# Weighted values of eight heads in one burst, twice a phase, in a two-layer transformer block kernel

## What is computed

```
x = x + attn0(layernorm(x))     # causal, rotary, scores q.k + 0.1 q^2.k^2, output projection with a gate
x = x + ffn0(layernorm(x))      # 128 -> 512, relu, -> 128, biases
x = x + attn1(layernorm(x))     # full attention, biases, no output projection
x = x + ffn1(layernorm(x))      # 128 -> 384 gate and up, silu(gate) * up, -> 128
attend: softmax(scores) @ V per head, 256 queries x 256 keys
```

## Time and profile before

| | us |
|---|---|
| median of three runs | 321.77 |
| the profiled execution | 320.94 |
| its span | 319.0 |
| PE busy | 292.7 |
| DVE busy | 252.6 |
| ACT busy | 217.0 |
| POOL busy | 176.8 |
| L978, the groups' products, busy | 61.7 |

### The profile page before, as it was taken

How to read it: one execution, slowest core, us unless ns; L and a number is a source line. 1 busy time by engine, 2 the same in 40 slices (tenths; PEclk the granted TensorE clock), 3 DMA queues, 4 the chain that set the end, 5 groups by cost and what they waited for, 6 DMA issues and landing times.

```text
span 319.0 us, 8438 instructions
## 1 busy us (share of the span) xinstructions
PE 292.7 (92%) x2852; PEld 209.1 (66%) x2852; DVE 252.6 (79%) x1000; ACT 217.0 (68%) x494; POOL 176.8 (55%) x406
## 2 busy tenths in 40 slices
PE   6769799899999999999999999999999999999945
PEld 4545566677776777777687766776666565655634
DVE  7878988987969877676777776779798989895464
ACT  7661566776676868685867767787778767677621
POOL 5642767778695868687777523527272717170210
PEclk9976799999999999999999999999999999999997
DMA  6977224411313121211212010021312111100001
GB/s 194 340 167 167 66 55 116 117 51 52 108 46 94 44 83 53 85 51 40 73 37 70 22 43 27 25 60 28 77 26 62 42 44 27 44 3 19 17 1 33
DMA packets 23178, 21.59 MB, mean 68 GB/s; under 512 B 2944, under 2 KB 20096, under 8 KB 23136
## 3 DMA queue, kind: packets, MB, share of 16 engines
q1 hardware_dynamic: 23136, 21.05, 23.9%
HBM read 13.18 MB, written 7.34 MB: 64 GB/s over the span
## 4 chain that ended last, share of the span: by engine, by line
PE 51%; DVE 25%; POOL 13%; issue 6%; ACT 4%; POOLq 0%; ACTq 0%; DVEq 0%
PE bank L978 11%; DVE NM L757 7%; PE bank L952 5%; PE bank L1008 4%; PE bank L1021 4%; PE bank L928 4%; POOL XN L430 3%; PE bank L929 3%; POOL RS L423 3%; POOL PB L469 3%; PE bank L956 3%; DVE JUNK L754 3%; PE bank L1067 2%; PE bank L1053 2%; PE bank L875 2%
## 5 line engine op out<-in xcount | busy, mean ns | idle before, releaser
L590 ACT ACTIVATE PB<-bank 128x384 f32<-128x384 f32 (+1 forms) x256 | 134.6, 545 | 47.7 <-PE bank L954 23.9
L757 DVE TENSOR_REDUCE NM<-bank 128x2 f32<-128x512 f32 x128 | 83.8, 684 | 21.0 <-PE bank L929 20.6
L952 PE MATMUL bank<-QS,KS 128*128 128x256 f16 x256 | 70.2, 275 | 2.4 <-ACT PB L590 1.6
L978 PE MATMUL bank<-PB,VP 128*32 128x256 f32 (+1 forms) x1024 | 61.7, 358 | 1.0 <-ACT PB L590 0.9
L754 DVE CUSTOM_DVE_ANT_0 JUNK<-bank,MSF 128x256 bf16<-128x256 f32 x128 | 53.7, 419 | 0.0
L752 DVE CUSTOM_DVE_ANT_0 JUNK<-bank,MSF 128x128 bf16<-128x128 f32 x128 | 36.3, 284 | 17.6 <-PE bank L926 17.5
L978 PEld LDWEIGHTS bank<-PB,VP 128*32 128x32 f32 x1024 | 26.7, 109 | 24.0 <-issue 9.5
L469 POOL TENSOR_SCALAR_AFFINE_SELECT PB<-PB 128x512 f32<-128x512 f32 x64 | 41.8, 654 | 0.0
L926 PE MATMUL bank<-KS,QS 96*128 96x256 f16 x128 | 35.8, 283 | 0.0
L928 PE MATMUL bank<-KS,QS 96*128 96x256 f16 x128 | 35.2, 275 | 0.4
L929 PE MATMUL bank<-KS,QS 96*128 96x256 f16 x128 | 34.6, 271 | 0.0
(11 more groups left out here) (101 smaller groups left out, 604.3 us busy)
## 6 DMA issues: line engine op xcount, KB each, us to landing
scr<-PR SPq DMA_DIRECT2D x16, 256.0 KB, 2.7
QS<-scr SPq DMA_DIRECT2D x16, 128.0 KB, 2.7
QS<-scr SPq DMA_DIRECT2D x32, 64.0 KB, 2.8
KS<-scr SPq DMA_DIRECT2D x32, 64.0 KB, 2.8
KS<-scr SPq DMA_DIRECT2D x16, 128.0 KB, 2.9
scr<-PR SPq DMA_DIRECT2D x16, 128.0 KB, 1.9
out_x<-xs SPq DMA_DIRECT2D x8, 128.0 KB, 1.9
W<-in_w SPq DMA_DIRECT2D x1, 576.0 KB, 5.9
```

Of the source, the lines that this page charges most:

```text
L590: act.activation(PB[:, s % RING, 0:n], scored(i, s)[:, 0:n], ACT.Exp).then_inc(s_e, 1)
L757: dve.tensor_reduce(m[:, s, 0:2], o[:, :].rearrange("q (n k) -> q n k", n=2), AX.X, ALU.max, negate=True).then_inc(s_mx, 1)
L952: pe.matmul(o[:, 0:S], k[:, 0:P], q[:, :], start=True, stop=True)
L978: ins = pe.matmul(o, v, pr, start=(g % 2 == 0 and kt == 0), stop=True, skip_group_check=True)
```

## The change

The groups are issued in pairs. In phases 0 to 14 groups 0 and 1 stand together at slot 10, and groups 2 and 3 at slot 2 of the next phase (slot 1 for layer 1). Phase 15 keeps slots 6, 10 and 14 and its last group. The ring of probabilities has 16 heads, and the exponentials wait for the same group of the phase before.

```diff
-RING = 8
+RING = 16
-PV = (6, 10, 14)
+def pv_groups(i, s):
+    if i == NPH - 1:
+        return {6: (0,), 10: (1,), 14: (2,)}.get(s, ())
+    return (0, 1) if s == 10 else ()
@@ exp (ACT)
-                if 4 * i + s // 4 >= 2:
-                    act.wait_ge(s_pv, 4 * i + s // 4 - 1)
+                if i > 0:
+                    act.wait_ge(s_pv, 4 * (i - 1) + s // 4 + 1)
@@ loop of PE
                     if s == last_pv_slot(i) and 0 <= i - 1 < NPH:
-                        pv(i - 1, 3)
+                        for g in ((3,) if i == NPH else (2, 3)):
+                            pv(i - 1, g)
...
-                    if s in PV and 0 <= i < NPH:
-                        pv(i, PV.index(s))
+                    if 0 <= i < NPH:
+                        for g in pv_groups(i, s):
+                            pv(i, g)
```

## The result

The changed kernel takes 335.25 us (median of 4 runs, 334.49 to 335.67), the one before 322.26 in the same series. The ratio is 1.0419, with a 95% interval of 1.0385 to 1.0454: slower, by 13 us. The forecast was 328.0 with a range of 320.5 to 331.5. The sign was right, the size was half of what came, and the range was missed.

The account below looks back on a forecast made before the run. PE, busy 92% of the span, was taken to set most of the time, not all. Joining groups 2 and 3, groups 0 and 1, and layer 1's terms summed to +6.2 us: 327.15 profiled, 328.0 median, range 320.5 to 331.5.

Parts of the forecast that it names:

- Cost of a group: Per group on PE: 0.88 us alone in layer 0, 1.10 in layer 1; 0.23 per visit; 0.65 and 0.87 as second.
- the signs that the forecast named: Longer PE wait before L875, longer phases 4 to 7, pairs of 1.59 and 2.07, L1021 waiting, DVE idle times moved.
- Group 2 is hidden in phases 3 to 8, and the move costs its whole time: Slot 14 gains nothing, PE waiting before L875; slot 2 adds 0.65 for phases 3 to 7, 0.87 for phase 8.
- Edit 2 in layer 0: Groups 0 and 1 together at slot 10: +0.1 us each in phases 4 to 8, +0.65 in phase 1, else 0.
- Layer 1, "Then slot 1 adds 0.87: +0.2 a phase": Phases 10 and 12 to 14: PE reaches slot 1 about 0.67 earlier, then pays 0.87; +0.8 for four phases.
- PE without a break: Phases 9 and 11: PE never idle, at most -0.46 each; with waits for ACT and DVE's maxima -0.2 each, -0.4 together.
- The first phases: Groups 2 and 3 joined: phase 0 zero, phases 1 and 2 +0.55; groups 0 and 1 joined: phase 1 +0.65.
- Edit 2 in layer 1, cost 0: Pair of groups 0 and 1 at slot 10: DVE's next work comes after 3.04, within 3.06; cost 0, at most 0.87.
- A: Rival: PE is the path everywhere, each of 30 visits saved gives 0.23; -6.9, 314.9 us; chance 0.12.
- B: Rival of no change: hidden group-2s cost 4.1, but every other joint pays; +0.2, 322.0 us; chance 0.20.
- C: Rival: the longer burst at slot 10 starves DVE and ACT; 6.1 more, 334.1 us; chance 0.08.

Follow-up runs that it names:

- g2_short: Kernel before the change with seven of the eight products of every group 2 left out (sums not the reference's); one run, 319.25 us.
- second_pair: Against the kernel before, only groups 2 and 3 joined, at slot 2 (1) of the next phase, with the 16-head ring; 331.82 us, ratio 1.033.
- first_pair: Against the kernel before, only groups 0 and 1 joined, at slot 10, with the 16-head ring; 326.99 us against 321.27, ratio 1.018.
- dn_bank6: Changed kernel with layer 1's down projection (product at slot 15) in bank 6 in place of 7; 333.49 us, ratio 1.0385 to the kernel before.
- l0_window: Against the kernel before, layer 0 with groups 0 and 1 at slot 14, 2 and 3 at the next phase's slot 2; 323.64 us, ratio 1.006.

## Why the forecast was right, and where it failed

- *Cost of a group.* 0.65 and 0.87 as a second, 0.23 per visit: the pairs measure 1.59 and 2.07 (270.33 to 272.40), as forecast to the hundredth. The short waits before the weight loads fell from 52 to 36. Right. Of the signs that the forecast named, all came but one: DVE has idle time at slot 0 of phases 12 to 14.
- *Group 2 is hidden in phases 3 to 8, and the move costs its whole time.* Right: the pairs of phases 3 to 7 stand at slot 2 of phases 4 to 8, and these grew by 0.72, 0.69, 0.70, 0.59 and 0.80, forecast 0.75 each (0.65 and the first pair's 0.1); g2_short and second_pair show it singly. Phase 9 takes in the pair of phase 8, forecast 0.87, and grew by 0.66: second_pair has 0.51 there, as its own group 2 gives back the 0.35 of g2_short, and first_pair 0.16.
- *Edit 2 in layer 0.* Right in size: first_pair costs -0.05 to 0.24 in phases 4 to 8, forecast 0.1; the changed kernel's L1027 at slot 8 waits for ACT's block, as said.
- *Layer 1, "Then slot 1 adds 0.87: +0.2 a phase".* This is the step that failed. The sentence before it says that without group 2 PE comes to slot 1 0.67 earlier. It did not ask what PE waits for at slot 15: the bank that DVE empties at slot 14. The list of waits of before has four such waits, 1.0 us together (L1067 for L823, quoted above), so short because group 2 stood before the product and filled the time. Without group 2 the wait of the weight loads grows from 0.25 to 0.68 in phases 12 to 14, the product starts no earlier against DVE, the 0.67 is 0, and the second group's 0.87 at slot 1 is paid in full. For phases 11 and 9 the forecast took "PE without a break" for "PE is the path" and counted group 2's time as gained: in phase 11 the same wait is 0.84 of idle time of PE in the changed kernel, and g2_short shows the group to be worth 0.05 there and 0.35 in phase 9. The pairs of phases 8 to 14 were to cost 1.27 (0.87 + 0.8 - 0.4), and phases 9 to 15, where their costs fall, pay 6.31 (0.66 + 5.65). So five of the eight us by which the profiles' difference missed the forecast are here. dn_bank6 gives back 0.57 in each of phases 10 and 12 to 14, 2.3 in all; in phase 11 the bank is read from the wait alone, since bank 6 is not free there.
- *The first phases.* The forecast had 1.2 for phases 0 to 3, measured 4.45 with the start. About 1.5 of it is the low clock in phase 1 (1.0 in the pair, 0.5 ahead of it), and first_pair and second_pair cost 1.2 and 0.6 in this phase without it; the three together come near the 3.4 of the phase. The profile of the kernel before has a low stretch of its own in phase 0, worth 1.1, so the 4.45 would be 5.5 against a profile without it. I had bounded each term by the time of one group, and not thought of PE's clock. Why first_pair pays 1.2 in phase 1 for the forecast 0.65 stays open.
- *Edit 2 in layer 1, cost 0.* In phases 12 to 14 of the changed kernel it adds nothing to the second pair, but in phase 11 it adds 0.51, and by itself it costs 0.47 to 0.50. In first_pair DVE idles 0.53 and 0.42 at slots 15 and 0, behind group 2 at slot 14. The forecast looked at the next slot alone (3.04 of 3.06), where DVE does not idle. That the two groups follow too closely is my reading; no run tests it. The 0 was luck in part, since the wait at slot 15 covers the cost.
- *Rivals.* A was right about the price of a visit and had no say in the time, as the visits saved stood where PE waits anyway. The rule of the Trainium skill that stands beside it ("TensorEngine Tiling (Array Packing)", Tiling Modes, Key Properties: a change of the tiling mode drains the engine) agrees with the trace, in the 0.23, and by itself says nothing of where the drain is hidden. B counted on gains of the joints that no phase from 4 on showed, but for 0.05 in phase 7 of first_pair. C had the best figure, 334.1, by luck: its reason fell, as no DVE idle time follows the pair at slot 10 of phase 12.

## What to carry to other kernels

An engine that is busy for 99% of a stretch may still have work in it that costs nothing, and a move of that work costs its full time at the new place. Before work is taken out of a place, look for every wait that follows it up to the next fixed point, the short ones too: a wait of 0.1 or 0.2 us is the visible end of one that the work itself fills. Then ask which engine ends that wait, and whether it would be earlier. The same holds for a move to another bank or buffer: it ends one wait and can bring another, which the work in front of it hides until that is moved too.

## What the runs showed of the chip

A stretch of low granted clock may stand at another place when waits move: the profile before has it for 3.4 us from 35.8 us, in phase 0, which then takes 17.05 in place of 15.9 to 16.0 in the profiles without it; the changed kernel has it at 60 us. In the three kernels with both pairs moved in phase 1 and the low stretch near 60 us, PE worked without idle time in it in the changed kernel (3.41 of 3.41 us busy), and in l0_window it idled 0.47 at its start (6.44 of 6.90 us busy).
